# A cleared tile and a wait in front of each of the 76 gathers of message rows

## The reference

```python
# each convolution; the first one's output goes through relu
msgs = x[src].reshape(n, 33, 128)
for t in range(33):
    g = msgs[:, t] @ wih.T + h @ whh.T + bih + bhh
    i, f, gg, o = split(g, 4)
    c = sigmoid(f) * c + sigmoid(i) * tanh(gg)
    h = sigmoid(o) * tanh(c)
out = h @ wl.T + bl + x @ wr.T
...
x = layernorm(x + conv2(relu(conv1(x))))
# relational layer
hr = einsum('ni,rio->rno', x, weight)
msg = hr[rel_type, src] * norm[:, None]
out = layernorm(x + relu(segment_sum(msg, dst, 512)))
```

## Time and profile before

| what | value |
|---|---|
| median of 3 runs | 528.29 us (525.88 to 530.48) |
| profiled execution | 528.7 us |
| its span, first to last instruction | 526.9 us |
| mean granted TensorE clock | 0.993 of full |
| busy: PE, DVE, ACT, POOL | 90%, 79%, 63%, 67% |
| POOL: 192 row gathers / 192 memsets / 76 message gathers | 198.7 / 65.3 / 78.3 us |

### The profile page before, as it was taken

The page is one execution under the profiler, slowest core; times in us unless marked ns, Lnnn a source line. Parts: engine busy times, 40 slices in busy tenths (PEclk is TensorE's granted clock), DMA queues, the critical chain, the costliest instruction groups (busy, mean ns, idle before and its releaser), DMA issues.

```text
span 526.9 us, 10326 instructions
## 1 busy us (share of the span) xinstructions
PE 475.9 (90%) x3599; PEld 359.4 (68%) x3599; DVE 414.5 (79%) x1134; ACT 334.5 (63%) x851; POOL 351.6 (67%) x478
## 2 busy tenths in 40 slices
PE   7599999999999779899999999999999887788775
PEld 3388887888888665688888888888855443344333
DVE  3579989989989864888888888889879766565655
ACT  2576776767677644677677777677756654555552
POOL 6568878787787732788888888786056556555650
PEclk9899999999999999999999999999999999989999
DMA  5855655565565532555555655555021111111110
GB/s 170 316 176 156 172 153 165 160 169 168 162 171 166 164 88 100 160 141 160 161 162 161 164 165 165 152 164 153 6 81 36 41 41 40 36 44 38 40 40 26
DMA packets 25907, 66.32 MB, mean 126 GB/s; under 512 B 6278, under 2 KB 10174, under 8 KB 25728
## 3 DMA queue, kind: packets, MB, share of 16 engines
q0 software_dynamic: 18048, 55.85, 37.6%
q1 hardware_dynamic: 6720, 8.89, 5.4%
q10 hardware_dynamic: 1088, 0.92, 0.5%
HBM read 62.48 MB, written 3.16 MB: 125 GB/s over the span
## 4 chain that ended last, share of the span: by engine, by line
PE 30%; DMA 22%; POOL 19%; issue 12%; DVE 10%; ACT 6%; DVEq 0%; SPq 0%; ACTq 0%; POOLq 0%
POOL rows L524 12%; PE gates L1240 11%; DMA edge_rows<-msg_table,msg_index 11%; DMA rows<-gate_table,src_steps 10%; POOL pause L522 5%; PE gates L1233 5%; PE work L1240 3%; PE work L1162 2%; DVE msg_full L1087 2%; PE gates L1185 2%; POOL edge_rows L537 2%; ACT msg_full L743 2%; PE work L1445 1%; ACT act_if L606 1%; PE work L1233 1%
## 5 line engine op out<-in xcount | busy, mean ns | idle before, releaser
L524 POOL DMA_INDIRECT rows<-gate_table,src_steps x192 | 198.7, 1035 | 53.7 <-POOL pause L522 50.5
L537 POOL DMA_INDIRECT edge_rows<-msg_table,msg_index x76 | 78.3, 1030 | 70.2 <-ACT msg_full L743 24.8
L1240 PE MATMUL gates<-h_hi,whh_hi 128*128 128x256 f16 x396 | 100.7, 273 | 4.1 <-ACT h_hi L596 2.5
L1240 PE MATMUL gates<-h_hi,whh_lo 128*128 128x256 f16 x396 | 100.4, 273 | 0.0
L600 ACT ACTIVATE act_if<-gates 128x512 f32<-128x512 f32 x96 | 57.5, 599 | 54.6 <-PE gates L1240 51.4
L522 POOL MEMSET pause<- 128x256 f32 x192 | 65.3, 340 | 33.1 <-DMA gate_table<-rows 19.0
L1233 PE MATMUL gates<-ident,rows 128*128 128x128 f32 x584 | 79.8, 273 | 7.0 <-issue 4.6
L1240 PE MATMUL gates<-h_lo,whh_hi 128*128 128x256 f16 x396 | 85.5, 274 | 0.4 <-DVE h_lo L885 0.4
L1233 PEld LDWEIGHTS gates<-ident,rows 128*128 128x128 f32 x584 | 66.9, 141 | 11.3 <-issue 5.9
L901 DVE TENSOR_TENSOR prod_fc<-act_if,cell 128x256 f32<-128x256 f32 x128 | 54.1, 422 | 23.7 <-ACT act_if L600 12.9
L1077 DVE TENSOR_SCALAR rows<-node_iota,dst_f 128x512 f16<-128x512 f16 x132 | 43.6, 364 | 30.7 <-ACT msg_full L743 29.2
(11 more groups left out here) (180 smaller groups left out, 993.3 us busy)
## 6 DMA issues: line engine op xcount, KB each, us to landing
rows<-gate_table,src_steps POOLq DMA_INDIRECT x192
gate_table<-rows SPq DMA_DIRECT2D x8, 256.0 KB
src_direct<-direct_rows SPq DMA_DIRECT2D x1, 2048.0 KB, 7.5
edge_rows<-msg_table,msg_index POOLq DMA_INDIRECT x76, 2.5
code<-code_table SPq DMA_DIRECT2D x6, 160.0 KB
msg_table<-table_sb SPq DMA_DIRECT2D x4, 192.0 KB, 1.9
code<-code_table SPq DMA_DIRECT2D x5, 128.0 KB
whhT<-turned_whh SPq DMA_DIRECT2D x2, 256.0 KB
```

The costliest lines, as they stand in the source:

```text
L524: pool.indirect_dma_start(target, None, table, bass.IndirectOffsetOnAxis(src_steps[:, t, k:k + 1], axis=0)).then_inc(landing(l, t, k)[0], 16)
L537: pool.indirect_dma_start(edge_rows[:, c % 2, n, :], None, msg_rows, bass.IndirectOffsetOnAxis(msg_index[:, pool_first(c) + n:pool_first(c ...
L1240: mm = pe.matmul(gate_place(t, h, gate), w[:, gate * P:(gate + 1) * P], state[:, h, :], start=(opens and opens_bank(t, gate) and n == 0), ...
```

## The change

In front of each of the 76 gathers of message rows, behind the waits that stand there, POOL clears the tile pause and waits until it is cleared, as it does in front of the row gathers. The semaphore paused counts on from the 192 of the row gathers (len(by_rows) * K); nothing reads the tile.

```diff
@@ -534,6 +534,8 @@
                     if pool_first(c) + n >= EDGES_UNDER_WAY:
                         landed, tile = asked[pool_first(c) + n - EDGES_UNDER_WAY]
                         pool.wait_ge(edge_rows_in[landed % 2][tile], 16 * slot_fills(landed, tile))
+                    pool.memset(pause[:, :], 0.0).then_inc(paused, 1)
+                    pool.wait_ge(paused, len(by_rows) * K + pool_first(c) + n + 1)
                     pool.indirect_dma_start(
                         edge_rows[:, c % 2, n, :], None, msg_rows,
                         bass.IndirectOffsetOnAxis(msg_index[:, pool_first(c) + n:pool_first(c) + n + 1], axis=0)
```

## The result

| kernel | median us (runs) | against before |
|---|---|---|
| before | 527.12 (20) | |
| changed | 529.98 (20) | 1.0062, interval 1.0041 to 1.0082 |
| before, second time | 524.99 (16) | |
| changed, second time | 529.85 (6) | 1.0100, interval 1.0058 to 1.0142 |

The change makes the kernel slower by 3.3 us (2.2 to 4.3) in the first comparison, by 5.3 (3.0 to 7.5) in the second. Differences in us are worked out from the ratios throughout, unless the text says otherwise.

A forecast was written before the change was run, and what follows sets the result against it. Landings of message gathers, two in flight, were taken to bound the stage. Terms 2.3 + 0.9 + 1.8 + 1.2 = +6.2 us on the profiled 528.7 gave 534.9, stated as 534.5 us for the lower median; range 530.0 to 538.5.

The forecast's parts named there:

- One wait: Gathers of blocks 1 and 2: landing-to-gather reaction grows from 0.30 to 0.63 us, 7 pairs, +2.3 us.
- Two waits: Gathers from block 3 on, landing awaited separately: reaction grows from 0.74 to 0.77 us, 30 pairs, +0.9 us.
- Memset against DVE: Message stage: 15 memsets collide with DVE's tensor_scalar at 0.17 us each, half paid, +1.2 us (0 to 4.3).
- the rule of the Trainium skill: Shared port pair of DVE and POOL: first issuer blocks the other; half of 0.35 us per caught memset, 4.4 us.
- The slack that is gone: Message gathers: both limits nearly equal, so a long gather delays both chains, +1.8 us (0 to 3.8).
- nearly free: Rival, message gathers: play between chains not used up, only reactions count, 1.7 to 3.2 us, say 530.8; chance 0.18.
- in full: Rival: gather comes up only after the memset, +0.60 on 37 reactions, +22 us, 550.5; chance 0.08 with other large costs.
- not slower: Rival, message stage: gathers moved later meet gaps of DVE, 526.6, or something else hides all, 528.3; chance 0.12.

## Why the prediction was wrong

**The rule was right.** Start at the later of the end of the gather before plus a gap and the landing of the second before plus a reaction: 0.60, 0.63 and 0.77 were read from the row gathers, and the message gathers show 0.60, 0.64 and 0.77. The exchange of the waits (-14 us, -9 by the stage, -10 expected), three in flight (-22, -24 expected) and the second memset (+28 to 30 on the changed kernel, +35 expected) came out in the order and nearly the size that the rule gives.

**The base was wrong.** The sum began at a profile whose message stage took 127.1 us. Four others took 123.8, within 0.2 of each other. The sum said of the gather of 3.28 us that it "stalls everything today as well" and kept it on both sides; it occurs in that one profile only, and the 528.3 us of three runs became 527.1 over twenty. The low end of the range, 530.0, was 528.3 + 1.7; on 527.1 it would have been 528.8, and 529.98 would lie inside. The middle would still have been too high: 6.2 us on the median of twenty is 533.3. The long gather was in a term as well: the excess of duration over 0.95 us is 6.1 us in the profile predicted from, and 1.8 to 3.4 in the four others, where the slack term reckoned with 3.8 beside the long one.

**The end was not one for one.** The sum let the stage's growth through to the end in full, with the time from the last gather to the end unchanged. It is 13.8 us in the profile predicted from but 14.7 in the other four of before, through PE's clock, and 13.7 to 13.8 changed: on the mean 0.75 of the 5.8 us of the stage do not arrive. The sum had nothing for this. That the stage grew by nearly the 6.2 of the sum is in part luck, since the terms, which follow, came out otherwise.

**One wait: +2.3 forecast, +3.2 by the profiles.** From landing to gather it is 0.26 in the kernel before where the landing is whole, not 0.30. The chain of waits in the second profile of before:

```profile
387.25 2.57 DMA edge_rows<-msg_table,msg_index
389.82 0.26 issue
390.08 2.52 DMA edge_rows<-msg_table,msg_index
392.61 0.26 issue
```

That makes the term 0.37 x 7 = 2.6; the longer eighth gather adds 0.6. The 3.2 hold the profile with the gather of 3.28 us; against the four others it is 3.8, of which 1.5 come up to the start of the eighth gather and 2.3 behind it. By time the 15 cost 2.3 (0.4 to 4.1). This term was sized well. The first gather, which the forecast had at +0.03, starts 0.99 us behind the landing of msg_table's store and not 0.74, because its memset takes 0.61: +0.25, in front of the stage.

**Two waits, slack and DVE: 0.9 + 1.8 + 1.2 = +3.9 forecast, +2.6 by the profiles, between -2.4 and +1.4 by time.** Here a term of the sum failed by its size. The reaction is right (0.74 to 0.77).

*Memset against DVE* is the step that fell, by the price of a collision and not by their number. In the four profiles of the changed kernel 17 to 21 of the 75 memsets behind the first start while the one-hot build (L1079, L1077 before) runs on DVE, where 15 were forecast. With the very first they take 0.36 us on the mean, the others 0.32 and never more than 0.33: a collision costs about 0.05 and not 0.17. In the first of the profiles ten take 0.35 to 0.39, one 0.45 and the very first 0.61; in the other three the longest behind the first are 0.49, 0.47 and 0.38. The price was read from one memset beside L814, which runs for 0.63 us; the one-hot build runs for 0.26 to 0.35 at a time. Summed up, the stretches behind the first are 0.4 to 0.7 us; if half of them is paid, as the prediction took it, the term is an estimated 0.2 to 0.4 us and not 1.2.

By the rule of the Trainium skill cited there (SBUF — State Buffer, "Who interferes with whom") the term was 4.4 us, further off still. The trace bears the rule out in part: every stretched memset of the four profiles started under the one-hot build. But about a quarter of the memsets is caught and not a third, and several of these show no stretch at all.

*The slack that is gone* was never measured by itself. That a late landing holds up both chains is seen in the starts: the largest distance over two gathers is 5.1 to 5.3 us in the profiles of the changed kernel, with 5.0 to 5.2 for its neighbour, and 4.0 to 4.7 before, mostly with a smaller neighbour (4.53 and 3.77 in the second profile). But the kernel with memsets in the first 15 alone shows 4.9 twice, too, and with the 61 memsets alone the time does not move by more than 1.4 us. So its 1.8 is the upper end; how much of it is real is not shown.

The rival "nearly free" (+1.7 to +3.2, 530.8) was closer to the time than the forecast; that is in part luck, for its 530.8 stands on the same base, 1.2 us too high. The rivals "in full" and "not slower" are excluded by the 0.77 and by the intervals.

**What stays open.** The stage grows by 5.8 us in nine profiles, the span by 4.7, the median time by 3.3 (2.2 to 4.3) and 5.3 (3.0 to 7.5) in two comparisons. Both intervals hold 1.0058 to 1.0082, 3.1 to 4.3 us. The LSTM part in front scatters by 3.5 us from profile to profile, as much as the whole effect, and nine profiles don't average that out. What makes a landing late or holds up the eighth gather, and why a short memset costs as much as a long one, stays open as well. I don't claim to know the price nearer than 3 to 5 us. The range of 530.0 to 538.5 took in the bounds of the terms but neither the scatter of the base nor a second look at it.

## What to carry to other kernels

Where a chain is paced by a latency with a few transfers in flight, write its rule down (later of two limits, each from a row) before costing an edit: here an added instruction was nearly free where it fitted inside the reaction, and cost its length or close to it where the other limit decided (3 to 5 us for the first memset, 17 with three in flight, 26 to 30 for the second). Look in what order an instruction's waits stand: putting the wait that is met last first in the code gave 14 us (9 of them in the stage), and one more transfer in flight 22, until PE was the limit. And never take the base of a sum from one profile: a single long instruction in it was worth half of the effect.

## What the runs showed of the hardware

With two waits in front of a gather on POOL, the order in the code decides how soon it starts: 0.74 us after the landing if the landing is awaited second, and some 0.3 if it is awaited first (worked out: the median distance from a start to the next but one is 2.83 us in the kernel with the waits exchanged, of which 2.5 are the landing; 0.26 is the figure with one wait alone). Behind a waiting instruction for the landing the gather takes 0.7 us to come up whether 0, 0.12 or 0.32 us of memset stand between (0.70; 0.07 + 0.12 + 0.54; 0.07 + 0.32 + 0.34). Three message gathers in flight land no later than two: the median from issue to landing is 2.5 us in both, ACT's wait for them almost vanishes (4.3 us for 30.4), and the gathers keep a mean of 1.0 us. A memset on POOL that starts while an f16 tensor_scalar (L1079) runs on DVE takes 0.36 us on the mean, 0.32 otherwise.
